# Experts as groups of 512 moving rows with the weights stationary, and 32-row tails on four column tiles

## Time and profile before

| | |
|---|---|
| median of 3 runs | 847.05 us |
| span of the profiled execution | 845.4 us |
| TensorE busy in it | 791.5 us (94%) |
| first matmul of an expert | 188.67 us |
| last matmul of an expert starts | 831.90 us |
| mean granted clock of TensorE | 0.970 |

### The profile page before, as it was taken

The page is one execution under the profiler, slowest core; times in us unless marked ns, Lnnn a source line. Parts: engine busy times, 40 slices in busy tenths (PEclk is TensorE's granted clock), DMA queues, the critical chain, the costliest instruction groups (busy, mean ns, idle before and its releaser), DMA issues.

```text
span 845.4 us, 13004 instructions
## 1 busy us (share of the span) xinstructions
PE 791.5 (94%) x3764; PEld 655.6 (78%) x3765; DVE 351.7 (42%) x791; ACT 318.6 (38%) x487; POOL 268.8 (32%) x313
## 2 busy tenths in 40 slices
PE   4999999628999999999999999999999999999993
PEld 3777888527888888888888888888888888888882
DVE  5886758685113621172216223511361172244111
ACT  6784755432214512262127125311441262262120
POOL 4346210003233422361216315322341262243311
PEclk9999999659999999999999999999999999999997
DMA  7247678628111811173116513712281164111111
GB/s 237 47 75 138 150 162 175 256 105 326 25 31 34 317 39 25 27 263 95 32 30 201 159 25 88 271 25 37 46 302 37 25 224 136 25 37 25 30 32 25
DMA packets 55873, 91.72 MB, mean 108 GB/s; under 512 B 7344, under 2 KB 40496, under 8 KB 49712
## 3 DMA queue, kind: packets, MB, share of 16 engines
q1 hardware_dynamic: 45728, 71.64, 27.2%
q0 software_dynamic: 9408, 19.42, 12.0%
q10 hardware_dynamic: 720, 0.46, 0.2%
HBM read 64.97 MB, written 18.15 MB: 98 GB/s over the span
## 4 chain that ended last, share of the span: by engine, by line
PE 86%; DVE 7%; DMA 2%; issue 2%; ACT 1%; POOL 0%; POOLq 0%; ACTq 0%; DVEq 0%
PE bank L720 23%; PE bank L718 23%; PE bank L719 23%; PE bank L734 4%; PE bank L631 3%; PE bank L632 3%; PE bank L633 3%; PE bank L712 2%; PE bank L653 1%; DMA xg<-xn_rows,gather_at 1%; DVE bn L782 1%; DVE wc_lo L823 1%; PE bank L671 1%; PE bank L646 1%; DVE mv L791 1%
## 5 line engine op out<-in xcount | busy, mean ns | idle before, releaser
L718 PE MATMUL bank<-w_hi,xT_hi 128*128 128x512 f32 x576 | 229.0, 398 | 4.3 <-DVE xT_lo L1019 4.3
L720 PE MATMUL bank<-w_hi,xT_lo 128*128 128x512 f32 x576 | 225.9, 392 | 0.0
L719 PE MATMUL bank<-w_lo,xT_hi 128*128 128x512 f32 x576 | 225.2, 391 | 0.0
L1042 DVE TENSOR_TENSOR h<-bank,h 128x512 f32<-128x512 f32 x72 | 49.8, 692 | 294.0 <-PE bank L720 293.8
L718 PEld LDWEIGHTS bank<-w_hi,xT_hi 128*128 128x128 f32 x576 | 108.9, 189 | 26.3 <-DVE xT_lo L1019 4.7
L720 PEld LDWEIGHTS bank<-w_hi,xT_lo 128*128 128x128 f32 x576 | 108.7, 189 | 23.4
L719 PEld LDWEIGHTS bank<-w_lo,xT_hi 128*128 128x128 f32 x576 | 108.9, 189 | 21.8
L718 PE MATMUL bank<-w_hi,hT_hi 128*128 128x512 f32 x288 | 118.7, 412 | 0.0
L559 ACT ACTIVATE h<-bank 128x512 f32<-128x512 f32 x72 | 43.1, 599 | 197.4 <-PE bank L720 197.4
L720 PE MATMUL bank<-w_hi,hT_lo 128*128 128x512 f32 x288 | 112.6, 391 | 0.0
L719 PE MATMUL bank<-w_lo,hT_hi 128*128 128x512 f32 x288 | 112.3, 390 | 0.0
(11 more groups left out here) (145 smaller groups left out, 924.2 us busy)
## 6 DMA issues: line engine op xcount, KB each, us to landing
w_raw<-in_units SPq DMA_DIRECT2D x48, 1024.0 KB, 5.9
joint<-xs_parts SPq DMA_DIRECT2D x64, 128.0 KB, 3.8
out_x<-XT SPq DMA_DIRECT2D x17, 256.0 KB, 3.6
XT<-in_x SPq DMA_DIRECT2D x16, 256.0 KB, 7.0
xn_rows<-xnb SPq DMA_DIRECT2D x16, 256.0 KB, 2.5
xg<-xn_rows,gather_at POOLq DMA_INDIRECT x37, 3.4
out_x<-y,add_at POOLq DMA_INDIRECT x36
gate_row<-gate_rows,gate_at POOLq DMA_INDIRECT x36
```

The lines of the kernel that those rows point to most:

```text
L718: pe.matmul(B[bank][:], stat_hi, hi, start=start, stop=False)
L719: pe.matmul(B[bank][:], stat_hi, lo, start=False, stop=False)
L720: return pe.matmul(B[bank][:], stat_lo, hi, start=False, stop=stop)
L1042: dve.tensor_tensor(h[:, j, :], B[2 * j + 1][:], h[:, j, :], ALU.mult).then_inc(h_out, 1)
```

## The change

All eight experts get a group of four columns (512 slots), written out one after the other without a loop. In a group the weights are stationary and the transposed tokens move, so that the first product gives the hidden values transposed as the second one needs them:

- `up(e, m)`, m 0 to 7: for each 128 hidden values 2 banks, each of 4 chunks x 3 matmuls of 128 x 512. `down(e, r)`, r 0 to 3: 8 chunks x 3 matmuls for the 128 slots r. That is 288 matmuls to an expert. `turn_h` is gone.
- The rows 513 to 544 of an expert are its tail: float32 matmuls of 32 rows straight from the raw weights, in which four pieces of the output go to the four partition quarters of a bank. `tail_products` issues 32 matmuls of 256 columns, `tail_parts` 8 of 512 columns, and `tail_joined` adds the four partial sums with one matmul by `folds`. These three are behind a branch on `tail_live`, which is set where the expert has more than 512 rows. The tail's gather, its transposes and its copies on ScalarE and VectorE are done for every expert.
- Rows past 544 are done by a loop behind all groups (`late_*`), again behind a branch.
- Four raw buffers take turns for all units in place of six. SP reloads one when the low half has been taken and the tail's matmul is past it (`tail_first`, `tail_second`; the semaphore is raised by the first matmul behind the tail).
- GpSimd takes no low half any more and copies no index; gathers and adds use fixed columns of the tables. Two y buffers. Each add waits for the one before it. The adds' destination rows and the order of gathers are fixed.
- The tables of tiles leave the path to the first matmul; their successor (`late_tables`) is made by VectorE in expert 1.

```diff
-            def turn_h(j): ...
-            def pe_tile(t, split): ...
+            def up(e, m, past=None):
+                n, j, cols = CHUNKS * e + m, m // 4, slice(P * (m % 4), P * (m % 4) + P)
+                if n >= 2:
+                    pe.wait_ge(h_out, n - 1)
+                for which in range(2):
+                    k = 2 * j + which
+                    if m % 4 == 0:
+                        pe.wait_ge(lo_ready[k], e + 1)
+                    bank = B[2 * (m % 2) + which][:]
+                    for c in range(4):
...
+                        ins = product(bank, (w_hi[k][:, c, cols], w_lo[k][:, c, cols]),
+                                      (xT_hi[:, c, :], xT_lo[:, c, :]), c == 0, c == 3)
+                    ins.then_inc(up_done, 1)
+            def down(e, r, past=None):
+                n, rows = GROUP * e + r, slice(P * r, P * r + P)
+                if n >= 2:
+                    pe.wait_ge(y_out, n - 1)
...
+                    if r == 0:
+                        pe.wait_ge(hT_lo_out, CHUNKS * e + m + 1)
...
+                    ins = product(bank, (hT_hi[:, m, rows], hT_lo[:, m, rows]),
+                                  (w_hi[k][:, c, :], w_lo[k][:, c, :]), m == 0, m == CHUNKS - 1)
+            def tail_products(e):
+                live = pe.value_load(tail_live[0:1, e:e + 1], min_val=0, max_val=1)
+                with pe.If_ne(live.val, 0):
+                    pe.wait_ge(tail_xT_out, e + 1)
...
+                    for c in range(4):
+                        for which in range(2):
+                            for g in range(4):
+                                raw = raw_of(e, 2 * (g // 2) + which)[0]
+                                pe.matmul(B[tail_banks(e)[which]][TAIL * g:TAIL * g + TAIL, 0:256], tail_xT[:, c, :],
+                                          raw[:, c, 256 * (g % 2):256 * (g % 2) + 256], start=c == 0, stop=c == 3)
+            def tail_parts(e):
...
+                    for b in range(2):
+                        for g in range(4):
+                            raw = raw_of(e, 4 + (2 * g + b) // 4)[0]
+                            pe.matmul(B[6][TAIL * g:TAIL * g + TAIL, :], tail_hT[:, b, TAIL * g:TAIL * g + TAIL],
+                                      raw[:, (2 * g + b) % 4, :], start=b == 0, stop=b == 1)
+            def tail_joined(e):
...
+                    pe.matmul(B[7][:], folds[:], y[0][:], start=True, stop=True)
+            for r in range(GROUP):
+                turn_tokens(0, r)
+            pe.wait_ge(xT_lo_out, GROUP)
+            for e in range(E):
+                for m in range(CHUNKS):
...
+                    up(e, m, past)
...
+                for r in range(GROUP):
+                    if e + 1 < E:
+                        turn_tokens(e + 1, r)
+                        if r == 1:
+                            tail_turn(e + 1)
+                        if r == 2:
+                            tail_products(e + 1)
+                            past = tail_first
+                        if r == 3:
+                            tail_turn_h(e + 1)
+                    down(e, r, past)
```

In experts 1 to 7 `tail_parts` follows `up(e, 1)` and `tail_joined` follows `up(e, 2)`; in expert 0 all steps of the tail lie behind `up(0, 0)` to `up(0, 4)`. The other engines:

```diff
             def load_unit(e, k):
+                n = UNITS * e + k
+                if n >= RB:
+                    before, unit = divmod(n - RB, UNITS)
+                    sp.wait_ge(lo_ready[unit], before + 1)
+                    sp.wait_ge(tail_first if unit < 4 else tail_second, before + 1)
...
             def gather_rows(e, r):
+                if e == 0:
+                    gather(xg_first[r], slots_of(src_i, e, r), xg_in[r])
+                    return
+                pool.wait_ge(xg_ps, r + 1 if n < GROUP + 2 else n - 1)
+                gather(xg[r % 2], slots_of(src_i, e, r), xg_in[r % 2])
...
+            pool.wait_ge(src_ready, 1)
+            for r in range(GROUP):
+                gather_rows(0, r)
...
+                for r in range(GROUP):
+                    if e + 1 < E and r < 2:
+                        gather_rows(e + 1, 2 + r)
+                    pool.wait_ge(y_out, GROUP * e + r + 1)
+                    if r:
+                        pool.wait_ge(y_st[(r - 1) % 2], 16 * (2 * e + (r - 1) // 2 + 1))
+                    else:
+                        pool.wait_ge(tail_st, 16 * (e + 1))
+                    add_rows(y[r % 2][:], slots_of(dst_i, e, r), y_st[r % 2])
...
+            def unit_high(e, k):
+                if e:
+                    act.wait_ge(*((up_done, 2 * CHUNKS * (e - 1) + CHUNKS * (k // 2 + 1) - 1 + k % 2) if k < 4 else
+                                  (down_done, GROUP * e)))
+                high_half(act, e, k)
```

More of the change, by code:

```diff
@@ L320, in _ @@
             sp.wait_ge(wc_lo_out, STEPS)
-            for k in range(UNITS):
+            for k in range(RB):
                 load_unit(0, k)
@@ L410, in gather_gates, with gather_gate @@
+            def gather_gate(row, index, landed):
                 pool.indirect_dma_start(
[L411 to L437, removed]
-                pool.indirect_dma_start(
[L439 to L443, removed]
@@ new lines, in gather_gate, with gather_gates, add_rows @@
+                    out=row, out_offset=None, in_=gate_dram,
+                    in_offset=bass.IndirectOffsetOnAxis(ap=index, axis=0)).then_inc(landed, 16)
+            def gather_gates(e):
+                if e >= 2:
+                    pool.wait_ge(y_out, GROUP * (e - 1))
+                for r in range(GROUP + 1):
+                    gather_gate(gate_row[e % 2][:, r:r + 1], slots_of(gate_i, e, r), gate_land[e % 2])
+            def add_rows(rows, index, landed):
+                pool.indirect_dma_start(
+                    out=out, out_offset=bass.IndirectOffsetOnAxis(ap=index, axis=0),
+                    in_=rows, in_offset=None, compute_op=ALU.add).then_inc(landed, 16)
@@ L761, in _, with product @@
-            turn_tokens(1)
-            pe_tile(0, 1)
-            pe.wait_ge(tables_ready, 1)
-            with pe.Fori(1, TILES) as t:
-                split = pe.value_load(tile_expert[0:1, bass.ds(t, 1)], min_val=0, max_val=E)
-                with pe.If_ne(split.val, 0):
-                    pe_tile(t, split)
+            def product(bank, stationary, moving, start, stop):
+                pe.matmul(bank, stationary[0], moving[0], start=start, stop=False)
+                pe.matmul(bank, stationary[0], moving[1], start=False, stop=False)
+                return pe.matmul(bank, stationary[1], moving[0], start=False, stop=stop)
@@ L1023, in _ @@
+            for r in range(GROUP):
+                tokens_low(0, r)
             dve.wait_ge(ex_out, 1)
@@ new lines, in _ @@
+            some = dve.value_load(late_any[0:1, 0:1], min_val=0, max_val=LATE_TILES)
+            with dve.If_ne(some.val, 0):
+                with dve.Fori(0, LATE_TILES) as i:
+                    live = dve.value_load(late_live[0:1, bass.ds(i, 1)], min_val=0, max_val=1)
+                    with dve.If_ne(live.val, 0):
+                        for j in range(2):
+                            dve.wait_ge(late_silu, i * 2 + (j + 1))
+                            dve.tensor_tensor(late_h[:, j, :], B[2 * j + 1][:], late_h[:, j, :], ALU.mult
+                                              ).then_inc(late_h_out, 1)
+                        dve.nop()
+                dve.nop()
```

666 lines of the change are left out of this document (453 added, 213 removed).

## The result

The changed kernel takes 775.74 us (median of four runs; three lie between 774.82 and 776.01, the fourth was an outlier at 4123 us, which the comparison leaves out). The kernel before took 848.03 in the same comparison. The ratio is 0.9145, 95% interval 0.9128 to 0.9162: 8.6% faster. Forecast were 780.9 with a range of 768 to 812.

What follows compares the result with a forecast made beforehand. The prediction took TensorE's instruction issue to bound the kernel. Its terms, from -70.9 for main matmuls to +32 for live tails, summed to -66.2 on the 845.4 us span, giving 779.2, or 780.9 us with 1.65 added; range 768 to 812.

Steps and rivals of the forecast that it cites:

- 1 four tiles less: Main matmuls, 2304 in place of 2592 at an unchanged 0.2266 us: four tiles of 17.73 us go, -70.9 us.
- 2, 5 hidden transposes out: In the experts: 64 hidden transpose groups go, -30.3 us; tail transposes done for every expert add +6.2.
- 2 token groups ahead of the start: Expert 0's four token transpose groups now lie ahead of the first matmul, 28 behind it instead of 32: -1.9 us.
- 4 second gather's wait: TensorE's stall for the second gather in the first tile disappears, -2.3 us.
- part 6: Live tails of experts 0, 1, 2 and 4: 8.0 us each, +32 in all, ends 24 and 86.
- part 3: Start: four gathers must land before the first matmul, which comes at 189.7, +1.0 us, bounds -2 to +5.
- part 7: End: register reads, index copies and the gate gather go, -3 us, bounds 0 to -4; the drain stays.
- Part 8: New waits on TensorE across the experts: 0.4 us an expert allowed, +3 us, bounds 0 to 18.
- B: Rival: column tiles stream one after the other, a live tail costs 21.4 us, total 834; chance 10%.
- D: Rival: each column-tiled record waits for the one before to drain, 48 us a live tail, total 942; chance 5%.
- E: Rival: expert rows above 544 would run the late loop, over 20 us a tile; chance 1%.
- C: Rival: the written-out schedule leaves TensorE waiting in each expert, +18 to +32 us, total 799 to 813; chance 14%.

Runs made afterwards that it cites:

- experiment 6: The kernel before with at most four tiles an expert, leaving out the four fifth tiles: 779.89 us, ratio 0.9200.
- Experiments 5: The kernel before with every group of four hidden-value transposes issued twice: 877.88 us, ratio 1.0359.
- experiment 4: The changed kernel with VectorE's low half of unit 1 moved behind the four tokens' low parts: 774.29 us, ratio 0.9130.
- experiment 1: The changed kernel with all four pieces of a tail's products and parts on the first column tile: 837.19 us, ratio 0.9875.
- experiment 7: The changed kernel with each float32r matmul of the experts cut to its first 256 moving columns: 612.20 us, ratio 0.7225.

## Why the prediction was right, step by step

All against the span, 845.4 to 774.3, which is -71.1 measured and -66.2 forecast.

| step | forecast | measured | from |
|---|---|---|---|
| 1 four tiles less, step 0.2266 | -70.9 | -70.9 | step 0.2267 after; experiment 6 |
| 2, 5 hidden transposes out, tail steps in, by expert | 8 x -3.0 = -24.1 | 8 x -3.10 = -24.8 | 67.83 against 70.93 |
| 2 token groups ahead of the start | -1.9 | -1.9 | same count, the forecast's price; not measured by itself |
| 3 start | +1.0 | +3.3 | 191.98 against 188.67 |
| 4 second gather's wait | -2.3 | -2.3 | none in the trace after |
| 6 live tails | 4 x 8.0 = +32 | 4 x 6.85 = +27.4 | 74.68 - 67.83 |
| 7 end | -3 | -1.9 | 11.58 against 13.48, from the start of the last main matmul |
| 8 new waits | +3 | about 0 | TensorE never idle from 197.2 |
| sum | -66.2 | -71.1 | |

The terms add up to the measured change, so nothing is left to explain beyond 0.1 us. A sum without terms agrees: from the first to the last main matmul are 643.23 us before and 570.74 after, -72.5, and the rows 1, 2, 4, 5 and 6 together give -72.5. That the total came out 5 us off and not 8 is in part luck: tails and waits were put 7.6 too high, start and end 3.4 too low.

**The mechanism was right where it mattered.** The time is the number of matmuls times the step, and swapping what is stationary left the step at 0.2267. Experiments 5 and 6 show in the kernel before that both savings are real path time: 0.43 us a group of transposes and 17.7 us a tile. The group saves by not running four tiles that held only 15, 17, 6 and 22 rows.

**The term that was mis-sized is the live tail, part 6.** I put it at 8.0 between 6.0 and 21.4, drawn up by the pair rate of 0.106 us in the earlier trace rows. That row is of a weight load of 128 columns. With 32 columns and four tiles, four pairs start within 20 ns and a round of four takes 0.216, what one record streams for. Which of the two lifts that rate was not tested apart. The lower bound was the answer: 3.59 + 1.85 + 0.86 = 6.3, and half a microsecond for the slower steps before and behind them.

The rule of the Trainium skill that spoke against it ("TensorE: Matmul & The Clock Gate", Part 3: a weight load overlaps a matmul in flight only when the row group differs) is not what the traces show: all four tiles here share their rows, and their loads and matmuls overlap, four pairs in 0.216 us. Of that section's other number, 2.38 times for three tiles, the runs have the pair for four: 13.93 / 3.59 = 3.9 times, better than the estimate from it, which was about three.

**The start, part 3, was wrong by 2.3 us.** I took 1.14 us for the first gather's issue from a row where VectorE did small steps beside it; the change puts a 2.29 us operation there (experiment 4). From the first gather's start to the fourth's are 5.55 us in place of the 4.3 that I had put, 1.3 of the 2.3. Another 0.4 lie ahead of the first gather (180.06 against 179.64), where executions scatter, and 0.6 behind the fourth: 6.4 to the first matmul in place of 5.8. The rows to look at were two others of the kernel before's timeline, a gather inside four low halves in a row:

```profile
189.66 8.89 DVE L270 TENSOR_TENSOR w_lo<-w_raw,w_hi 128x2048 fp32r<-128x2048 f32 x4
...
196.66 2.74 POOL L404 DMA_INDIRECT xg<-xn_rows,gather_at  x1 [0.27 <-POOL gather_at L455]
```

The Trainium skill states a contention that fits ("GPSIMD Engine Reference", 8, Key points): GpSimd shares its interfaces to SBUF with VectorE and contends with operations of two SBUF inputs. `low_half` is one, and 2.71 against 1.14 us agrees; the gate gather of 0.94 us under another low half does not, so what else it takes stays open.

**The end, part 7, by 1.1.** The register reads went (2.3 us became 0.56), but the gate gather had lain beside the add's own landing and drain, 9.6 and 9.7 us in the two kernels. I had taken it off the path without asking what ended last.

**Part 8 and the rivals.** Part 8 was put at +3 and came out at about 0. No wait that the change adds reaches TensorE. The tightest place I named, the tail's chain at r 3, held. B is refuted by experiment 1, D by the 3.59 us of the changed kernel's own products, E by the trace, in which no late matmul stands. C isn't there at 512 columns and appears with 256 (experiment 7), and with it come stretches at half clock.

## What to carry to other kernels

When one engine issues all the time, price a change by the distance of its instructions' starts, in the forms that stay, and add up; a listed duration or a busy share would have misled here. A last tile with few rows costs a full tile: choose what moves so that whole groups fill it, and give the leftover rows their own cheap form, with matmuls of different column tiles next to each other in the queue. And before calling an instruction at the end or the start cheaper, look at what else runs beside it in its new place.

## What the runs showed that I had not expected

- Four column tiles of 32 run at 3.9 times one for float32 with 256 columns (13.93 / 3.59) and at 3.8 times with 512 (6.98 / 1.85). The order in the queue decides: in turn 3.59 us, eight records to a tile 8.10, four to a tile 1.87 (against 1.85).
- A large VectorE operation (128 x 2048, 2.29 us) beside GpSimd's issue of an indirect DMA lengthened it from 0.96 or 1.14 us to 2.71, but not each issue beside one (0.94 at 648.39).
- TensorE stood at half clock for the first 5.2 us of the experts, after a stretch in which it mostly waited. Useless matmuls over the 10 us ahead of them brought the granted clock to 1.00 and the total down by 2.5 to 3.2 us (774.29 to 771.05, two sittings).
- Waits can cost twice. Behind the second gather's wait the granted clock was 0.50 for 3.4 us with 3.11 us of waiting (experiment 6) and also with 1.92 (experiment 5), but not with the 2.18 of the kernel before; the many waits of experiment 7 gave 34 us of it.
- A float32r matmul with 128 weight columns costs 13.3 ns beside its columns, at 512 and at 256: 6% of TensorE's time in the experts. A float32 record with 32 weight columns costs 2.7.
